# Attention halves with an earlier reciprocal and later waits, and a two-level histogram, in a four-layer graph kernel

## The reference

```python
h = jnp.maximum(_layernorm(x, axis=-1), 0.0)
x = x + _L0_gnn_ref(h, adj, ...)     # two graph products, then four small LSTMs over windows of 1 to 4 nodes
h = jnp.maximum(_layernorm(x, axis=-1), 0.0)
x = x + _L1_gnn_ref(h, adj, W, a)    # attention with leaky scores s1_i + s2_j, masked by adj
h = jnp.maximum(_layernorm(x, axis=-1), 0.0)
x = x + _L2_gnn_ref(h, adj, Wqkv, Wo)  # causal attention, adj added to the scores
h = jnp.maximum(_layernorm(x, axis=-1), 0.0)
x = x + _L3_gnn_ref(h, adj, W1, b1, W2, b2)
# L3: d = deg^-1/2;  L_norm = d (diag(deg) - adj) d;  _, U = eigh(L_norm)
#     out = U @ (relu((U.T @ features) @ W1 + b1) @ W2 + b2)
```

## Time and profile before

| | |
|---|---|
| runs | 930.72 us median of 3 (925.45 to 931.0) |
| profiled execution | 927.66 us, of which the recorded span is 925.9 us |
| PE / PEld busy | 788.0 us (85%) / 518.8 us (56%) |
| DVE busy | 729.3 us (79%), 3418 instructions |
| ACT busy | 502.9 us (54%) |
| POOL busy | 163.2 us (18%) |
| mean granted TensorE clock | 0.959 of full speed |

### The profile page before, as it was taken

One profiled execution on the slowest core, in us unless ns is written; L12 is line 12 of the kernel. 1 busy time (PEld: TensorE's weight loads), 2 busy tenths in 40 slices (PEclk: granted clock), 3 DMA queues, 4 the chain that ended last, 5 costly groups with the idle time before them and its releaser, 6 DMA issues. The chain is left out here.

```text
span 925.9 us, 13739 instructions
## 1 busy us (share of the span) xinstructions
PE 788.0 (85%) x3736; PEld 518.8 (56%) x3736; DVE 729.3 (79%) x3418; ACT 502.9 (54%) x1106; POOL 163.2 (18%) x397
## 2 busy tenths in 40 slices
PE   3569998999999999999999996588873787788898
PEld 2358775444444466666554555466653565566665
DVE  6877676888888788888888788959789989869533
ACT  0027885665444434444444441378763776697675
POOL 2111111111121111111111110012102332070000
PEclk9999998999999999999999998799996988999999
DMA  9000000000000000000000000000000000000122
GB/s 281 27 1 1 1 2 0 1 0 1 1 1 1 1 0 1 1 1 2 0 1 1 0 1 1 1 1 1 1 1 0 1 1 0 1 1 1 36 79 69
DMA packets 13970, 12.16 MB, mean 13 GB/s; under 512 B 1091, under 2 KB 10822, under 8 KB 13894
## 3 DMA queue, kind: packets, MB, share of 16 engines
q1 hardware_dynamic: 10704, 8.46, 3.1%
q10 hardware_dynamic: 3190, 2.84, 1.0%
HBM read 7.10 MB, written 4.19 MB: 12 GB/s over the span
## 5 line engine op out<-in xcount | busy, mean ns | idle before, releaser
L565 ACT ACTIVATE G<-bank,bias 128x512 f32<-128x512 f32 (+1 forms) x252 | 159.1, 634 | 192.7 <-PE bank L662 170.7
L662 PE MATMUL bank<-HT,wih 128*128 128x512 f32 (+1 forms) x504 | 248.5, 579 | 0.4 <-ACT HT L551 0.4
L432 POOL TENSOR_TENSOR col_root<-sa,neg_half 128x1 f32<-128x1 f32 x126 | 69.0, 548 | 450.1 <-DVE sa L907 450.1
L662 PE MATMUL bank<-H,whh 128*128 128x512 f32 (+1 forms) x288 | 135.0, 551 | 1.4 <-DVE H L905 0.8
L521 ACT ACTIVATE T<-X,nbias,rstd 128x128 f32<-128x128 f32 x256 | 104.6, 485 | 4.9 <-DVE nbias L906 4.9
L525 ACT COPY T<-bank 128x512 f32<-128x512 f32 x128 | 74.9, 585 | 56.2 <-PE bank L662 41.6
L662 PEld LDWEIGHTS bank<-VI 128*128 128x128 f32 x254 | 47.4, 202 | 72.9 <-DVE VI L905 46.4
L662 PEld LDWEIGHTS bank<-HT,wih 128*128 128x128 f32 x504 | 80.0, 193 | 9.9 <-issue 3.9
L662 PEld LDWEIGHTS bank<-XI,A 128*128 128x128 f32 x252 | 43.1, 201 | 73.6 <-DVE A L906 67.0
L672 PE MATMUL bank<-ident,T 128*128 128x128 f32 x256 | 41.1, 291 | 50.6 <-ACT T L608 43.1
L906 DVE SCALAR_TENSOR_TENSOR XI<-xy,bank 128x2 f32<-128x2 f32 x125 | 28.2, 225 | 55.2 <-PE bank L662 49.2
(11 more groups left out here) (344 smaller groups left out, 1667.3 us busy)
## 6 DMA issues: line engine op xcount, KB each, us to landing
out_x<-T SPq DMA_DIRECT2D x16, 256.0 KB, 2.3
wih<-in_WihT ACTq DMA_DIRECT2D x1, 1024.0 KB
whh<-in_WhhT ACTq DMA_DIRECT2D x1, 1024.0 KB
qkvT<-in_WqkvT ACTq DMA_DIRECT2D x1, 192.0 KB
wg<-in_Wg ACTq DMA_DIRECT2D x2, 64.0 KB
l3w<-in_L3W ACTq DMA_DIRECT2D x2, 64.0 KB
adjT<-in_adjT ACTq DMA_DIRECT2D x1, 64.0 KB
adj<-in_adj SPq DMA_DIRECT2D x1, 64.0 KB, 2.2
```

The costliest lines, as they stand in the source:

```text
L432: e.tensor_tensor(out=col["root"][:, :], in0=sa[:, 0:1], in1=neg_half[:, :], op=ALU.pow).then_inc(root_ready, 1)
L565: e.activation(G[x.h][:, gate, 0:n], gate_bank(k)[:, 0:n], ACT.Tanh if gate == 2 else ACT.Sigmoid, bias=bias[:, 4 * (x.p - 1) + gate:4 * ( ...
L662: mm = lambda out, l, r, start=True, stop=True: e.matmul(out, l, r, start=start, stop=stop)
```

## The change

- `add_output` no longer makes the reciprocal. `inverse_sums(before)` makes it for group k-1 in the scores half of k, ahead of the row maximum of k, with no wait behind it; it first waits for the exponentials of k-1. Group 31 has its own in its output half.
- Each of the four additions to `X` signals, and each `bn_stats` waits for its own addition alone; the last `bn_stats` of `add_output` and of `residual` is not waited for. PE's waits on `g_x` and `q_x` count four for a group.
- The waits for the sums that signal `lull` and `p_done` come behind the halves.
- `stats_1` issues its three first operations without waits and squares the difference without one.
- The histogram has two levels. DVE compares the 128 limits with the last point's count of each partition (`below`, 128x128); PE sums that over partitions and spreads it. DVE makes a one-hot matrix of the block in which each eigenvalue lies (`block_hot`), PE picks that block's 32 counts and its index (a new POOL iota in `cnt`), and three small DVE operations finish `cnt1`. Both products lie in slot `HIST_IN` = 10, behind the scores of the next group and ahead of `turn_next`.

```diff
-HIST_AFTER = max(S for S in SLOTS if needs(S) <= block_ends()[NB - 1] + 2)
+HIST_IN = slot_of_block(NB - 1)
...
-        hist, compare, prodL = sb("hist", [P, P]), sb("compare", [P, P * POINTS[0]], BF16), sb("prodL", [P, KB * 2 * POINTS[-1]])
+        below, block_hot, prodL = sb("below", [P, P]), sb("block_hot", [P, P]), sb("prodL", [P, KB * 2 * POINTS[-1]])
...
+            e.iota(cnt[:, POINTS[0]:POINTS[0] + 1], pattern=[[0, 1]], base=0, channel_multiplier=1, allow_small_or_imprecise_dtypes=True).then_inc(s_pool, 1)
+            e.wait_ge(s_pool, 11)
...
-                        e.wait_ge(g_x if earlier.gat else q_x, earlier.g + 1)
+                        e.wait_ge(g_x if earlier.gat else q_x, GB * (earlier.g + 1))
...
+                if S == HIST_IN:
+                    e.wait_ge(hist_in, 1)
+                    mm(bank[7][:, 0:P], ones[:, :], below[:, :]).then_inc(hist_ps, 1)
+                    e.wait_ge(hist_in, 2)
+                    mm(bank[7][:, ds(P, POINTS[0] + 1)], block_hot[:, :], cnt[:, 0:POINTS[0] + 1]).then_inc(hist_ps, 1)
...
-                if S == HIST_AFTER:
-                    e.wait_ge(hist_in, 1)
-                    mm(bank[7][:, 0:1], hist[:, :], ones[:, 0:1]).then_inc(hist_ps, 1)
...
-                net(TT(mean[:, o], stat[:, o, 1], stat[:, o, 4], ALU.add))
-                net(TT(dm[:, o], stat[:, o, 1], stat[:, o, 4], ALU.subtract))
-                net(TT(var[:, o], stat[:, o, 2], stat[:, o, 5], ALU.add))
+                e.wait_ge(ch_n, net.n)
+                differences = net.note(TT(dm[:, o], stat[:, o, 1], stat[:, o, 4], ALU.subtract))
+                squares = net.note(TT(var[:, o], stat[:, o, 2], stat[:, o, 5], ALU.add))
+                net.note(TT(mean[:, o], stat[:, o, 1], stat[:, o, 4], ALU.add))
+                e.wait_ge(ch_n, differences)
+                net.note(TT(dm[:, o], dm[:, o], dm[:, o], ALU.mult))
...
+                e.wait_ge(ch_n, squares)
                 net(TS(var[:, o], var[:, o], 1.0 / D, EPS, ALU.mult, ALU.add))
-                net(TT(dm[:, o], dm[:, o], dm[:, o], ALU.mult))
                 net(STT(var[:, o], dm[:, o], 0.25, var[:, o], ALU.mult, ALU.add))
                 e.reciprocal(out=var[:, o], in_=var[:, o]).then_inc(stats_in, 1)
...
-                net(r)
-
-            def add_output(g, es, os_, xs):
+                net.note(r)
...
+            def inverse_sums(x):
+
+                m = sm[x.g % 2]
+                e.wait_ge(g_e if x.gat else q_e, x.g + 1)
+                return net.note(e.reciprocal(out=m[:, 12:16], in_=m[:, 8:12]))
+
+            def add_output(g, inverted, os_, xs):
 
                 m, bk = sm[g % 2], bank[3 * (g % 2):]
-                e.wait_ge(es, g + 1)
-                net(e.reciprocal(out=m[:, 12:16], in_=m[:, 8:12]))
+                e.wait_ge(ch_n, inverted)
                 e.wait_ge(os_, g + 1)
                 for b in range(GB):
                     xb = X[:, g * GB + b, :]
-                    i = STT(xb, bk[1][:, ds(b * P, P)], m[:, 12 + b:13 + b], xb, ALU.mult, ALU.add)
-                i.then_inc(xs, 1)
-                e.wait_ge(xs, g + 1)
-                for b in range(g * GB, (g + 1) * GB):
-                    r = rows(b)
-                net(r)
+                    STT(xb, bk[1][:, ds(b * P, P)], m[:, 12 + b:13 + b], xb, ALU.mult, ALU.add).then_inc(xs, 1)
+                for b in range(GB):
+                    e.wait_ge(xs, g * GB + b + 1)
+                    r = rows(g * GB + b)
+                net.note(r)
...
-                x = Group(k)
+                x, before = Group(k), Group(k - 1)
+                if kind == "scores" and before:
+                    inverted[before.k] = inverse_sums(before)
+                if kind == "output" and k == GROUPS - 1:
+                    inverted[k] = inverse_sums(x)
...
-                    add_output(x.g, g_e, g_o, g_x)
+                    add_output(x.g, inverted[k], g_o, g_x)
...
                             TT(pb[:, s + 2], t, u[s % 2], ALU.add).then_inc(p_done, 1)
-                            e.wait_ge(p_done, n + 1)
                         elif half_next:
                             pauses += 1
                             TT(pb[:, s + 2], t, u[s % 2], ALU.add).then_inc(lull, 1)
-                            e.wait_ge(lull, pauses)
                         else:
                             rec(TT(pb[:, s + 2], t, u[s % 2], ALU.add))
                         for _i in range(half_next):
                             attentions(halves)
                             halves += 1
+                        if s == KB - 1:
+                            e.wait_ge(p_done, n + 1)
+                        elif half_next:
+                            e.wait_ge(lull, pauses)
...
-                    cv = compare[:, :].rearrange("p (k f) -> p k f", f=f)
-                    link(TT(cv, cnt[:, 0:f].unsqueeze(1).to_broadcast([P, P, f]), limit_row[:, :].unsqueeze(2).to_broadcast([P, P, f]), ALU.is_le))
-                    e.tensor_reduce(out=hist[:, :], in_=cv, axis=AX.X, op=ALU.add).then_inc(hist_in, 1)
+                    TS(below[:, :], limit_row[:, :], cnt[:, f - 1:f], None, ALU.is_ge).then_inc(hist_in, 1)
                     e.wait_ge(hist_ps, 1)
-                    link(e.tensor_copy(out=c("cnt1"), in_=bank[7][:, 0:1]))
+                    TS(block_hot[:, :], bank[7][:, 0:P], float(P - 1), cnt[:, f:f + 1], ALU.min, ALU.is_equal).then_inc(hist_in, 1)
+                    e.wait_ge(hist_ps, 2)
+                    link(TS(red[:, 0:f], bank[7][:, ds(P, f)], limit[:, :], None, ALU.is_le))
+                    link(e.tensor_reduce(out=c("cnt1"), in_=red[:, 0:f], axis=AX.X, op=ALU.add))
+                    link(STT(c("cnt1"), bank[7][:, P + f:P + f + 1], float(f), c("cnt1"), ALU.mult, ALU.add))
```

More of the change, by code:

```diff
@@ L413, in _ @@
             e.iota(grid[:, :], pattern=[[1, POINTS[0]]], base=0, channel_multiplier=POINTS[0], allow_small_or_imprecise_dtypes=True).then_inc(s_pool, 1)
-            e.wait_ge(s_pool, 10)
+            e.iota(cnt[:, POINTS[0]:POINTS[0] + 1], pattern=[[0, 1]], base=0, channel_multiplier=1, allow_small_or_imprecise_dtypes=True).then_inc(s_pool, 1)
+            e.wait_ge(s_pool, 11)
             for t, op, base, cm, st in ((ident, ALU.is_equal, 0, 1, -1), (low, ALU.is_gt, 0, 1, -1), (upper, ALU.is_gt, 0, -1, 1), (sup, ALU.is_equal, -1, -1, 1)):
@@ L890, in _ @@
                     if g == 1:
-                        e.wait_ge(q_x, NG)
+                        e.wait_ge(q_x, GB * NG)
                     mm(last_bank(g, 1)[:, :], l3w1[:, :], T[g % 2][1][:, :]).then_inc(r_s1, 1)
@@ L1034, in att_scores @@
                 e.tensor_reduce(out=sm[g % 2][:, 4:8], in_=half4(bank[3 * (g % 2) + 2]), axis=AX.X, op=ALU.max, negate=True).then_inc(q_m, 1)
+            inverted = {}
             def attentions(h):
                 kind, k = HALF[h] if h < N_HALVES else ("none", 0)
-                x = Group(k)
+                x, before = Group(k), Group(k - 1)
[3 more added lines that the diff above has]
+                    inverted[k] = inverse_sums(x)
                 if kind == "scores" and x.gat:
@@ L1044, in attentions @@
                 if kind == "output" and x.gat:
-                    add_output(x.g, g_e, g_o, g_x)
+                    add_output(x.g, inverted[k], g_o, g_x)
                 if kind == "output" and not x.gat:
-                    add_output(x.g, q_e, q_o, q_x)
+                    add_output(x.g, inverted[k], q_o, q_x)
                 if kind == "stats_1":
```

## The result

| | before | after |
|---|---|---|
| median of the runs compared | 928.12 us (4 runs, 925.45 to 931.0) | 913.45 us (4 runs, 913.16 to 918.57) |
| ratio of the runs | 1 | 0.9848, 95% interval 0.980 to 0.9896 |
| profiled execution / span | 927.66 / 925.9 us | 918.57 / 916.9 us |
| mean granted TensorE clock | 0.959 | 0.960 |

The kernel is 1.5% faster. The medians lie 14.7 us apart and the forecast saving was 14.5. The forecast of 916.0 is 2.6 us above the measured 913.45, and that is the base: it was made on the median of three runs, 930.72, and with the fourth run before has 928.12.

The account below looks back on a forecast made before the run. DVE was taken to set the pace from 563 us on, with the path leaving it for POOL, ACT and PE in places. Stage savings summed to 14.5 us, taking the median from 930.72 to 916 us, range 909 to 923.

Parts of the forecast that it names:

- The cost of a waited operation: In DVE's pairs of halves, dropped waits save 0.24, 0.11 and 0.12 us, 0.47 for a full pair.
- Residual stage: From 563 us, DVE the bound: 15 tails of 0.12 and one stats_1 of 0.6 save 2.4 us.
- The stats_1 within the tridiagonalisation: One stats_1 between DVE's own steps saves 0 to 0.6 us, taken as 0.3.
- Histogram: From the counts' reduction to the first operation on cnt1, 10.27 us before: saves 5.5 us, between 4.5 and 6.
- Pass 0: Three full pairs and two tails ahead of ACT's signs save 1.9 us; gains from there to the counts are lost.
- Pass 1: Pairs and tails from output 9 on save 2.7 us; outputs 12 and 18 win nothing, held by POOL's product.
- 826 to the last groups: From 826 to 854 us, DVE the bound again: one tail and three outputs at 0.35 save 1.2 us.
- from Z to the end: From the evaluation of the eigenvectors on: ACT's 0.64 us wait for the last stats_1 goes, saving 0.6 us.
- 799 to 826: Maxima of group 23 start later behind the reciprocal while ACT idles: 0.1 us lost; the rest is ACT and PE.
- my slower rival: The maxima's new wait for the previous group's exponentials costs up to 25.8 us, giving 942 us; chance 0.03.
- Only the histogram pays: Early starts fail or other engines take them back; only 5.5 us saved, giving 925.2 us; chance 0.12.
- The stretches called lost pay too: Savings in stretches counted as lost in waits also pay: 20 us saved, about 911 us; chance 0.20.

Follow-up runs that it names:

- recip_behind: Changed kernel with the reciprocal of k-1 issued behind the row maxima of k, still without a wait between them: 916.29 us, 0.9887 of the kernel before.
- lull_first: Changed kernel with the waits for the sums that signal lull and p_done back ahead of the halves: 912.95 us, 0.9856 of the kernel before.
- tails_back: Changed kernel with add_output again waiting for all four additions before the first statistic, and for the last statistic: 917.24 us, 0.9889 of the kernel before.
- waits_only: Changed kernel with the old one-level histogram back at the end of slot 11: 922.38 us, 0.9922 of the kernel before.
- hist_late: Changed kernel with its two histogram products at the end of slot 11, where the old product stood: 920.96 us, 0.9910 of the kernel before.
- hist_only: Kernel before with the two-level histogram and its products in slot 10 alone, every other line as before: 921.29 us, 0.9916 of the kernel before.
- after_again: Changed kernel, unedited, timed and profiled a second time: 915.30 us, 0.9846 of the kernel before.
- product_memset: Changed kernel with POOL's products of neighbouring terms replaced by same-size fills, so signs and eigenvalues are not computed: 902.09 us in one run.
- after_third: Changed kernel, unedited, timed and profiled a third time: 912.92 us, 0.9852 of the kernel before.
- hist_early: Changed kernel with both histogram products right behind slot 10's sums, ahead of the next group's scores: 912.51 us, 0.9853 of the kernel before.
- early_and_first: Changed kernel with histogram products ahead of the next group's scores and POOL's neighbour product ahead of the next block's table: 910.51 us, 0.9820 of the kernel before.

## Why the prediction was right

**The cost of a waited operation: right, and a little low.** A pair won 0.52 to 0.54 for 0.47, and its parts 0.26, 0.12 and 0.14 for 0.24, 0.11 and 0.12. All three edits carry their own share of a pair, as the timelines of recip_behind, lull_first and tails_back show. The Trainium skill's rule (VectorE: DVE Perf Modes, The DRAIN you can't avoid), by which dropped semaphores between chained operations win nothing, is contradicted for these short operations by the 0.52 and by waits_only's 0.9922; the same section adds that an operation which isn't held starts earlier, and the 0.20 for 0.32 agrees with that.

**Residual stage: 2.5 us measured, 2.4 forecast.** 15 tails won 2.0 for 1.8, and stats_1, from its first operation to its last, 0.50 for 0.6: that term was a little large. The stats_1 within the tridiagonalisation saved some 0.5 (forecast 0.3). **Histogram: 5.88, 5.5 forecast**, since PE reached the first product 0.3 us sooner behind the counts than taken from the earlier trace rows. hist_late shows that the place was the right thing to cost.

**Pass 0: 1.9 forecast, 2.4 to 2.8 between the traces, but part of that is PE's clock.** From X of 6 to X of 7 the kernel before took 8.76 us at a granted clock of 0.81, and so did the first profile of the changed kernel, with 9.01; behind X of 7 the clock was 0.91 in the one and 1.00 in the other. hist_only, with none of the new waits, took 7.27 from X of 6 to X of 7 at 1.00, and after_again 7.53 at 1.00. These two agree in the clock of the whole pass to 0.01 (0.92 and 0.91 ahead of X of 6, 0.90 and 0.89 behind X of 7), and between them the pass takes 84.06 and 82.97: the new waits saved 1.1 us at a like clock, and my term was too large. That everything behind ACT's signs up to the counts is lost in waits holds there: from X of 5 to the counts hist_only takes 30.45 and after_again 30.36.

**Pass 1: 2.4 in the first profile, 1.6 to 1.7 in the other two, 2.7 forecast.** Between these, too, a step of the clock changes the reading: X of 19 to X of 20 took 7.20 us at 1.00 in the first profile and 8.68 at 0.80 in the others, which win part of it back at output 15. That output 12 wins nothing because POOL's product holds DVE came out to the hundredth; product_memset shows that this is the cause. Some of the rest was lost in longer waits for PE: DVE's at outputs 15 and 20 grew by 0.9 and 0.7 us.

**826 to the last groups: 1.4 for 1.2,** and in the two later profiles 0.7 to 0.8 for 0.6 from Z to the end, where ACT no longer waits for the last stats_1. In the first profile that stretch lost 0.9. There it took 5.15 us from X of 31 to ACT's square root at a granted clock of 0.71, and 3.61 at 1.00 in the other two.

**799 to 826: wrong.** I forecast a loss of 0.1 us (the maxima of 23 start 0.1 later), and the stage lost 0.9 to 1.5, all between X of 24 and X of 25. The first candidate was the new wait, my slower rival, which does happen there: the maxima now come behind the exponentials. DVE of the changed kernel:

```profile
813.17 0.18 DVE L1022 RECIPROCAL sm<-sm 128x4 f32<-128x4 f32 x1 [3.52 <-ACT T L609]
813.26 0.66 DVE L1044 TENSOR_REDUCE sm<-bank 128x4 f32<-128x512 f32 x1
...
817.37 1.13 DVE L909 SCALAR_TENSOR_TENSOR X<-bank,sm,X 128x128 f32<-128x128 f32 x4 [3.45 <-PE bank L663]
```

The maxima of 26 do come behind the exponentials of 25, as the earlier trace rows let me expect. But the output at 817.37 waits for PE, and PE is slow. PE of the changed kernel:

```profile
813.19 1.00 PE L673 MATMUL bank<-ident,T 128*128 128x128 f32 x4 [2.47 <-ACT T L609]
813.98 1.92 PE L663 MATMUL bank<-T,mqk 128*128 128x512 f32 x2
815.69 1.57 PE L663 MATMUL bank<-H,T 128*128 128x128 f32 x8
```

and of lull_first, which has the same new wait:

```profile
814.53 0.66 PE L673 MATMUL bank<-ident,T 128*128 128x128 f32 x4 [2.48 <-ACT T L609]
815.02 1.11 PE L663 MATMUL bank<-T,mqk 128*128 128x512 f32 x2
815.98 1.16 PE L663 MATMUL bank<-H,T 128*128 128x128 f32 x8
```

The same products take 4.1 us from the first start to the end in the one and 2.6 in the other, behind the same idle time of 2.47 and 2.48 us. lull_first and tails_back, both of the second set, keep the new wait and have 8.17 and 8.16 in this interval, the length of the kernel before; so has product_memset. recip_behind, where the maxima of 26 come ahead of the wait again, has 8.16 too. The granted clock of these stretches is 0.57 in the changed kernel (813.2 to 817.2, mostly at 1.2 GHz) and 1.00 (2.4 GHz) in lull_first. So the wait by itself costs nothing, as the prediction had it for group 26, and the 0.9 to 1.5 us is PE's clock, for which the prediction had no term. The seven kernels with the new waits in the other two sets have 9.1 to 9.7, after_third among them, which was the rival's sign in that run; the kernel before has 8.16, and so has hist_only of the first set. So on the chip of set 1 the lower level went together with the new waits, and on that of set 2 it didn't. What decides between the levels at this place, the chip or the few tenths by which the stages shifted, stays open.

**The ends of the program: not forecast.** Ahead of 563 us the changed kernel took 1.5 to 3.2 us longer, though its stats_1 there saved some 0.5. The loss lies between 300 and 350 us. The window of the first profile and, below it, that of hist_early:

```profile
300.00:350.00 50.00, 47.80 (x181) 29.51 (x180) 37.99 (x208) 19.08 (x34) 8.89 (x24) 0.90 0.00 1
```

```profile
300.00:350.00 50.00, 46.73 (x196) 28.91 (x196) 40.70 (x224) 21.25 (x39) 9.58 (x26) 1.00 0.00 1
```

The granted clock is 0.90 here and 0.93 in after_again and after_third; the profile of before had 1.00. It is 0.93 in hist_only, which has none of the new waits, and in waits_only, which has none of the new histogram. And it is 1.00 in hist_early, whose program is that of the changed kernel up to slot 10: there the first stage took 560.98 us, 1.6 less than before. On the same chip after_third took 564.11. Over the eleven traces in which the first stage's text is that of the changed kernel it took 560.1 to 567.0. So one and the same text comes with the loss and without it. What decides it stays open.

Executions of one kernel lie 3 to 8 us apart in the timed runs too (906.96 to 910.59 for early_and_first, 907.41 to 915.85 for after_third). That such steps of the clock make up the spread fits, but isn't shown: by its mean granted clock a run can't be placed (of after_third's, 907.41 and 914.16 both have 0.966). The profiled execution of the changed kernel, 918.57, is the longest of its four; the others have 913.2 to 913.6. That is most of why the single profiled pair (9.1 us) reads as less than the medians (14.7).

**Where luck came in.** That the saving missed by only 0.2 us is partly luck. Terms that were too large (both passes, a stats_1) and the unforeseen 0.9 to 1.5 us behind X of 24 stood against terms that were too small (a pair, the histogram, the tails of the residual stage), and by the medians the two later comparisons gave 13.2 and 13.3. What is borne out beyond that is the sum behind the first stage, 14.2 forecast and 12.2, 14.2 and 14.0 measured, and the cost of each edit in the timelines.

**The other rivals.** "Only the histogram pays" would have been a saving of 5.5 and fell to waits_only. "The stretches called lost pay too" would have needed 20 us; output 12's zero and the unchanged 19.2 us from the second counts to X of 24 speak for the stretches being pinned, and so does X of 5 to the counts, which won 0.1 between hist_only and after_again.

## What to carry over

A wait between two short operations in one engine's queue cost 0.12 to 0.15 us at each place here, and all such places together were 0.8% of the time; look for the last of several identical signals, for a wait that could stand behind independent work, and for a small independent operation to lay between a producer and its consumer. When work is taken off an engine at a hand-over, look at the other engine's queue: the lighter histogram was worth nothing at the old place and 5.9 us at an earlier one. Before a stretch is called lost or won, find whether another engine's shared port or wait ends it, and compare several profiles, with the granted clock of the same stretch in each, before a difference of one or two microseconds is explained: here five stretches changed by 0.9 to 3.5 us with the clock alone.

## What the runs showed of the hardware

- An operation on 128x128 f32 that must wait for its forerunner starts 0.32 us behind it, one that needn't 0.20; a small one 0.21 against 0.09.
- DVE's product of two SBUF inputs took 1.18 us beside a POOL product of two inputs and 0.27 beside a fill by POOL.
- After the same 2.5 us of idle time the same matmuls ran at 0.66, 1.11 and 1.16 us in one execution and 1.00, 1.92 and 1.57 in another. In hist_early and in early_and_first an idle time of 1.11 us on PE ahead of the histogram's products was followed by a product of 2.05 and 2.06 us that takes 1.02 in the changed kernel.
- Between the same two events the same work took 7.20 us at a granted clock of 1.00 and 8.68 at 0.80 (X of 19 to X of 20), 7.53 and 9.01 at 1.00 and 0.81 (X of 6 to X of 7), and 3.61 and 5.15 at 1.00 and 0.71 (X of 31 to the square root).
- At the lower clock a hand-over from DVE to PE and back costs more too: 0.73 us idle on DVE in hist_early, with PE's product of 0.64 in it, and 0.50 in the changed kernel, with one of 0.41.
